# Causal attention heads with on-chip turned probabilities: 32x32 block turns, an on-chip exchange and a plain 32-bit value product

## The chip, the core and the metric

The kernel runs on one core of one Trainium2 chip. A core has TensorE (PE: matmuls and transposes into PSUM), VectorE (DVE), ScalarE (ACT), GpSimd (POOL, which has no access to PSUM) and SyncE (SP), which here only issues DMAs. Each engine runs its own list of instructions in order and waits on semaphores. The metric is the time of one execution on the device, in microseconds (us).

## What is computed

The input `x` has 2 batches of 1024 rows of 256 values. Two blocks follow each other. The first is one causal attention of width 256. The second is a transformer layer: causal attention with 16 heads of width 128 with rotary embedding, and then a mixture of 4 experts of which 2 are taken per row. The part on which the change works is the attention, in both blocks:

```python
scores = jnp.einsum('bhqd,bhkd->bhqk', q, k) / math.sqrt(HD)
scores = jnp.where(causal[None, None], scores, jnp.finfo(jnp.float32).min)
probs = jax.nn.softmax(scores.astype(jnp.float32), axis=-1)
out = jnp.einsum('bhqk,bhkd->bhqd', probs, v)
out = out.transpose(0, 2, 1, 3).reshape(b, s, H * HD)
return out @ wo + bo
```

Everything is 32-bit floating point. In the kernel most products are made of three cheaper ones: each operand is split into a high and a low part of the type `fp32r`, and high x high, high x low and low x high are added up in PSUM.

## The kernel before

The work is cut into 34 units. Units 0 and 1 are the first block's attention for the two batches, units 2 to 33 are one head of one batch each (`unit_of(p, b, h)`: pair of heads, batch, half). A unit has 8 query tiles of 128 rows; tile i needs key tiles 0 to i. So 36 tiles of 128x128 probabilities belong to a unit, and they are treated in two chunks c of 4 query tiles.

For a head unit u the steps are:

- `project_q(u, x)`, x = 0 to 3: TensorE makes queries and keys (two chunks each, 6 matmuls of 512 columns). ScalarE adds the bias (`add_bias`, L1152), SyncE swaps the two halves of the 128 partitions for the rotation with two DMAs (`swap`, L2555 and L2556), VectorE multiplies by the cosine (`rotate`, L1738), GpSimd multiplies by the sine and adds (`turn`, L2296 and L2300), ScalarE writes the high part (`high_qk`, L1158) and GpSimd the low part (`low_qk`, L2307).
- `scores(u, i)`: TensorE, into one or two of the four banks of `ps_s`. VectorE adds the causal mask and takes the maximum (`row_max`, L1777), ScalarE takes the exponential from PSUM into `prob_s` or `prob_b` and its row sum (`exponent`, L1194).
- `transposes(u, i)`: TensorE turns the i + 1 tiles of probabilities, one instruction a tile (L608), into the two banks of `ps_t`. ScalarE copies them out as high part (`high_p`, L1201), VectorE as low part (`low_p`, L1784).
- `outputs(u, c)`: TensorE multiplies the values by the turned probabilities, three matmuls a key tile (12 for chunk 0, 24 for chunk 1). ScalarE and VectorE split the result (`high_o` L1210, `low_o` L1790), `out_project` multiplies it by the output weights (6 matmuls of 256 columns, four times a unit), and VectorE adds it to `acc` (`accumulate`, L1817).
- `project_v(s, g)`: values for the next unit (12 matmuls of 256 columns), split by ScalarE (`high_values`, L1163) and VectorE (`low_values`, L1745).

`take_bank` hands out the two banks of `ps_m` in turn for all but scores and transposes, and waits until the last user's bank has been read.

The order of all this is written out by hand, engine by engine: a `start()` for units 0 to 2, `head(u)` for u = 3 to 30 (28 units, the same list each time, with weight loads that depend on r = (u - 2) mod 4), and an `ends()` for units 31 to 33, the experts and the output. In `head(u)` the scores, maxima and exponents of tiles 4 to 7 of unit u and of tiles 0 to 3 of unit n = u + 1 stand together. TensorE's list in it is:

```python
transposes(u, 0); scores(u, 4); transposes(u, 1); scores(u, 5)
project_q(n, 0); out_project(u - 1, 1, 0)
transposes(u, 2); transposes(u, 3); scores(u, 6)
out_project(u - 1, 1, 1); project_q(n, 1); outputs(u, 0)
transposes(u, 4); project_q(n, 2); out_project(u, 0, 0)
scores(u, 7); transposes(u, 5); out_project(u, 0, 1)
project_q(n, 3); project_v(v_next, 2 * half_of(u)); scores(n, 0)
transposes(u, 6); scores(n, 1); scores(n, 2); scores(n, 3)
transposes(u, 7); project_v(v_next, 2 * half_of(u) + 1); outputs(u, 1)
```

Of the kernel before, what the change touches and what calls it, by code (L numbers as in the profile page):

```python
# [14 lines left out]
P = 128  # L15
BATCH, T, D = 2, 1024, 256
NT = T // P
# [48 lines left out]
VALUES = values_of(LAST) + 1  # L66
QK_JC = ((0, 0), (1, 0), (0, 1), (1, 1))
TG = [[i + 1] if i < 4 else [4, i - 3] for i in range(NT)]
LN_VECTORS = (0, 0, 1, 1, 2, 2)
# [37 lines left out]
def build(nc, A):  # L107

    with ExitStack() as ctx:
# [43 lines left out]
        v_hi = sb("v_hi", [P, 2, NT, D], F32R)  # L153
        v_lo = sb("v_lo", [P, 2, NT, D], F32R)
        pT_hi = sb("pT_hi", [P, NT, CH], F32R)
        pT_lo = sb("pT_lo", [P, NT, CH], F32R)
# [23 lines left out]
        rows = sb("rows", [P, TC, D])  # L180
        hf = sb("hf", [P, KD, CH])
# [25 lines left out]
        t_groups = [(u, i, j) for u in range(UNITS) for i in range(NT) for j in range(len(TG[i]))]  # L207
# [81 lines left out]
        v_hi_done = event("v_hi_done", v_groups)  # L289
        v_lo_done = event("v_lo_done", v_groups)  # L290
# [4 lines left out]
        t_hi = event("t_hi", t_groups)  # L295
        t_lo = event("t_lo", t_groups)
# [74 lines left out]

        def t_bank(u, i, j):
            return ps_t[:, t_mm.place[u, i, j] % 2, :]
# [11 lines left out]
        def we_dst(m, e, n):  # L385
            x = ((qk_hi, qk_lo), (v_hi, v_lo))[m - 1][n]
            whole = x[:, 0].rearrange("p a n -> p (a n)")
            return whole[:, e * CH:(e + 1) * CH]
# [4 lines left out]
        def we2_part(n, e, k):  # L393
            return (v_hi, v_lo)[n][:, 0, 2 * e + k, :]
# [4 lines left out]
        def mid_part(n, u, i):  # L399
            if u == END_MID:  # L400
                return (pT_hi, pT_lo)[n][:, i, :]
# [10 lines left out]
        def m_bank(*use):  # L412
            return ps_m[:, shared[use] % 2, :]
# [15 lines left out]
        def _(pe):  # L429
            freed = {"gate": gate_got, "sums": gate_out, "pv": o_lo, "pvs": acc_done, "wo": acc_done, "mid": gelu_done}  # L430

            def take_bank(*use):

                n = len(shared)
                if n >= 2:
                    kind, *key = list(shared)[n - 2]
                    if kind == "q":
                        empty = first_lo if key[0] < 2 else cos_done
                    elif kind == "v":
                        empty = v_lo_done  # L440
                    elif kind == "ln":
                        empty = hT_hi_act
                    elif kind == "fold":
                        empty = None
                        pe.wait_ge(fold_lo[key[0]], 1)
                    elif kind == "bob":
                        empty = None
# [2294 lines left out]
```

## Time and profile before

| | us |
|---|---|
| median of 3 runs (lowest, highest) | 1116.75 (1116.45, 1118.06) |
| span of the profiled execution | 1115.4 |

The median lies 1.35 us above the profiled span. In the profile, busy times are sums over an engine, "PE" is TensorE's matmuls and "PEld" its weight loads, which run beside them. Matmul records overlap: each lasts from its issue to the end of its pipeline, so what one matmul costs is the distance from its start to the next one's start, not its duration. In a merged row of k equal matmuls the distance is (length of the row - length of one) / (k - 1). A plain 32-bit matmul appears as two records. Which engine waits for which is in the waits at the end of a row, and how the 16 DMA engines are filled is a share of their common time.

### The profile page before, as it was taken

How to read it: one execution, taken by the hardware profiler on the slowest of the kernel's cores; microseconds unless marked ns; L12 is line 12 of the kernel's file. 1: busy time of each engine (PE TensorE's matmuls, PEld its weight loads, DVE VectorE, ACT ScalarE, POOL GpSimd, SP SyncE). 2: the span in 40 equal slices, each digit the busy share in tenths (PEclk: the TensorE clock that was granted, in tenths of full speed). 3: DMA queues.
4: the chain of work that ended last, by engine and by line, in shares of the span. 5: the costliest groups of instructions: out<-in, count | busy, mean ns of one | idle time of the engine just before them, and what ended most of it. 6: DMA issues, size and time to landing. Idle time of an engine off the chain costs nothing.

```text
span 1115.4 us, 20396 instructions
## 1 busy us (share of the span) xinstructions
PE 1105.2 (99%) x7100; PEld 1006.7 (90%) x7100; DVE 834.9 (75%) x1978; ACT 748.3 (67%) x1584; POOL 638.1 (57%) x516
## 2 busy tenths in 40 slices
PE   9999999999999999999999999999999999999997
PEld 8999899999999999999999999999999999988897
DVE  7776777777777777777777777777777777977776
ACT  5666867666666666666666666666666666688765
POOL 2217666555555555555555555555555556777676
PEclk9999999999999999999999999999999999999999
DMA  5002412121212121212121212121211212230102
GB/s 176 1 1 62 129 39 53 39 62 39 52 39 62 39 53 39 60 39 50 37 60 39 52 39 62 39 48 44 62 38 37 50 40 57 48 110 14 39 1 76
DMA packets 33285, 56.54 MB, mean 51 GB/s; under 512 B 5792, under 2 KB 10016, under 8 KB 33184
## 3 DMA queue, kind: packets, MB, share of 16 engines
q1 hardware_dynamic: 33040, 55.21, 19.9%
q8 instruction: 57, 0.93, 0.3%
q14 instruction: 44, 0.36, 0.1%
q10 hardware_dynamic: 144, 0.03, 0.0%
HBM read 17.47 MB, written 4.19 MB: 19 GB/s over the span
## 4 chain that ended last, share of the span: by engine, by line
PE 95%; POOL 2%; issue 1%; ACT 1%; DMA 1%; DVE 1%; SPq 0%; POOLq 0%; ACTq 0%; DVEq 0%
PE ps_m L458 58%; PE ps_s L458 23%; PE ps_t L608 12%; PE ps_m L505 1%; DMA work<-in_attn_w 0%; POOL acc L2341 0%; POOL qk_lo L2346 0%; PE ps_m L479 0%; POOL wqk_lo L2346 0%; PE ps_t L458 0%; POOL pT_lo L2354 0%; DMA work<-work 0%; POOL acc L2330 0%; PE ps_m L666 0%; PE ps_m L667 0%
## 5 line engine op out<-in xcount | busy, mean ns | idle before, releaser
L2296 POOL TENSOR_TENSOR work<-work,rope 128x512 f32<-128x512 f32 x128 | 165.5, 1293 | 222.8 <-DMA work<-work 222.7
L1784 DVE TENSOR_TENSOR pT_lo<-ps_t,pT_hi 128x512 fp32r<-128x512 f32 (+3 forms) x408 | 210.8, 551 | 32.7 <-ACT pT_hi L1201 30.2
L1201 ACT ACTIVATE pT_hi<-ps_t 128x512 fp32r<-128x512 f32 (+3 forms) x408 | 182.8, 489 | 65.3 <-PE ps_t L608 65.1
L1777 DVE CUSTOM_DVE_ANT_0 ps_s<-ps_s,causal 128x128 f32<-128x128 f32 (+7 forms) x272 | 203.5, 767 | 6.7 <-PE ps_s L458 4.1
L2300 POOL TENSOR_TENSOR work<-work 128x512 f32<-128x512 f32 x128 | 167.6, 1310 | 10.0
L2307 POOL TENSOR_TENSOR qk_lo<-work,qk_hi 128x512 fp32r<-128x512 f32 x128 | 163.0, 1293 | 17.8 <-ACT qk_hi L1158 17.8
L1152 ACT ACTIVATE work<-ps_m,bqk 128x512 f32<-128x512 f32 x128 | 88.8, 694 | 116.5 <-PE ps_m L458 116.4
L1817 DVE SCALAR_TENSOR_TENSOR acc<-ps_m,rinv,acc 128x256 f32<-128x256 f32 x272 | 118.6, 478 | 63.0 <-PE ps_m L458 61.7
L1194 ACT ACTIVATE prob_b<-ps_s,nmax 128x640 f32<-128x640 f32 (+3 forms) x136 | 130.3, 958 | 17.9 <-DVE nmax L1777 14.6
L458 PE MATMUL ps_s<-qk_hi 128*128 128x384 f32 (+5 forms) x384 | 140.6, 366 | 0.0
L1738 DVE SCALAR_TENSOR_TENSOR work<-ps_m,bqk,rope 128x512 f32<-128x512 f32 x128 | 95.5, 746 | 54.3 <-ACT work L1152 54.0
L458 PE MATMUL ps_m<-pT_lo,v_hi 128*128 128x512 f32 (+3 forms) x384 | 132.6, 345 | 0.0
L458 PE MATMUL ps_m<-pT_hi,v_lo 128*128 128x512 f32 (+3 forms) x384 | 132.6, 345 | 0.0
L458 PE MATMUL ps_s<-qk_lo,qk_hi 128*128 128x384 f32 (+5 forms) x384 | 131.5, 343 | 0.0
L458 PE MATMUL ps_s<-qk_hi,qk_lo 128*128 128x384 f32 (+5 forms) x384 | 130.9, 341 | 0.0
L458 PE MATMUL ps_m<-pT_hi,v_hi 128*128 128x512 f32 (+3 forms) x384 | 130.1, 339 | 0.0
L608 PE MATMUL ps_t<-ident,prob_b 128*128 128x128 f32 x884 | 120.1, 274 | 0.4 <-DVE pT_lo L1784 0.4
L608 PEld LDWEIGHTS ps_t<-ident,prob_b 128*128 128x128 f32 x884 | 99.7, 140 | 9.8 <-issue 1.2
L458 PE MATMUL ps_m<-hT_hi,wqk_hi 128*128 128x512 f32 x256 | 103.6, 405 | 0.0
L1158 ACT ACTIVATE qk_hi<-work 128x512 fp32r<-128x512 f32 x128 | 79.1, 641 | 36.4 <-POOL work L2300 36.3
L458 PE MATMUL ps_m<-hT_lo,wqk_hi 128*128 128x512 f32 x256 | 101.0, 395 | 0.0
L458 PE MATMUL ps_m<-hT_hi,wqk_lo 128*128 128x512 f32 x256 | 100.5, 393 | 0.0
(235 smaller groups left out, 2822.7 us busy)
## 6 DMA issues: line engine op xcount, KB each, us to landing
work<-work SPq DMA_DIRECT2D x256, 128.0 KB, 2.3
wst<-in_head_qk SPq DMA_DIRECT2D x16, 256.0 KB, 2.9
acc<-in_x_tiles SPq DMA_DIRECT2D x8, 256.0 KB, 6.8
wo_st<-in_L_ffn_wo SPq DMA_DIRECT2D x16, 128.0 KB, 2.4
wst<-in_pair_v SPq DMA_DIRECT2D x8, 256.0 KB, 3.0
x_rows<-acc SPq DMA_DIRECT2D x4, 512.0 KB, 3.6
wst<-in_expert SPq DMA_DIRECT2D x8, 256.0 KB, 3.0
rope<-x_rows SPq DMA_DIRECT2D x4, 512.0 KB, 4.1
```

The lines of the kernel that those rows point to most:

```text
L458: ins = pe.matmul(out, lhs[x], rhs[y], start=first and k == 0, stop=last and k == 2)
L608: last = pe.transpose(t_bank(u, i, j)[:, k * P:(k + 1) * P], probs(i)[:, part], ident[:, :])
L1152: act.activation(qb[:, x % 2, :], m_bank("q", u, x), ACT.Identity, bias=bqk[:, j, head_:head_ + 1]).then_inc(qb_done.sem, qb_done.up(u, x))
L1194: act.activation(probs(i), all_scores[:, score_range(i)], ACT.Exp, bias=nmax[:, u % 2, i:i + 1], scale=-1.0, accum_out=rsum[:, u % 2, i:i ...
L1201: act.activation(pT_hi[:, slots, cols], t_bank(u, i, j)[:, 0:size * P].rearrange("p (j q) -> p j q", q=P), ACT.Copy).then_inc(t_hi.sem, t_ ...
L1738: dve.scalar_tensor_tensor(qc[:, ring3(u, x), :], m_bank("q", u, x), bqk[:, j, head_:head_ + 1], cos_t[:, c * CH:(c + 1) * CH], ALU.add, A ...
L1777: dve.tensor_tensor_reduce(s, s, causal[:, T - (i + 1) * P:T], -1.0, ABOVE_ALL, ALU.add, ALU.min, accum_out=nmax[:, u % 2, i:i + 1]).then_ ...
L1784: dve.tensor_tensor(pT_lo[:, slots, cols], t_bank(u, i, j)[:, 0:size * P].rearrange("p (j q) -> p j q", q=P), pT_hi[:, slots, cols].bitcas ...
L1817: last = dve.scalar_tensor_tensor(acc[:, b, tile, :], src[:, t * D:(t + 1) * D], rinv[:, u % 2, tile:tile + 1], acc[:, b, tile, :], ALU.mu ...
L2296: pool.tensor_tensor(qs[:, x % 2, :], qs[:, x % 2, :], sin_t[:, c * CH:(c + 1) * CH], ALU.mult).then_inc(sin_done.sem, sin_done.up(u, x))
L2300: pool.tensor_tensor(qc[:, ring3(u, x), :], qc[:, ring3(u, x), :], qs[:, x % 2, :], ALU.add).then_inc(rope_done.sem, rope_done.up(u, x))
L2307: pool.tensor_tensor(qk_lo[:, u % 2, j, cols], qc[:, ring3(u, x), :], qk_hi[:, u % 2, j, cols].bitcast(F32), ALU.subtract).then_inc(qk_lo_ ...
```

## The change

For the 28 units of `head(u)` (`TURNED`, u = 3 to 30) the transposes on TensorE go, with the copies that follow them:

- `exponent` writes a row's probabilities stepped: key 128 j + 4 k + g goes to place 128 j + 32 g + k, in runs over g with a step of 32 elements.
- `turn_probs(u, i)`: VectorE transposes each 32x32 block of query tile i (4 (i + 1) blocks per 32 partitions, one instruction a tile) into a buffer `turned[c]`.
- `exchange(u, c)`: SyncE moves the blocks between partitions with four DMAs, from 32 partitions to 128 each: 4 x 256 KB for chunk 0 and 4 x 512 KB for chunk 1, from `turned[c]` to `moved[c]`, 3 MB a unit.
- `early_outputs(u)` (chunk 0) and `far_outputs(u, 0)`, `far_outputs(u, 1)`, `near_outputs(u)` (chunk 1) take the place of `outputs`. Chunk 1 of unit u is multiplied in `head(u + 1)`, or at the head of `ends()` for unit 30.

In all units the value product is one plain 32-bit matmul a key tile instead of three; values and probabilities are no longer split, so `low_p` and `low_values` go, and the copies to SBUF are whole (`copy_p`, `copy_values`). Units 0 to 2 and 31 to 33 still transpose on TensorE. In `head` the two banks of `ps_t` join those of `ps_m`, and `take_bank` takes them in turn. The lists of all engines in `head` are written in another order.

```diff
+            def block_product(u, c, j, last):
+                s, h, off = values_of(u) % 2, half_of(u), max(0, j - TC * c) * Q4
+                out = by_quarter(m_bank("pv", u, c))[:, :, off:P]
+                probs_ = moved[c].rearrange("p (g j n) -> p g j n", g=4, n=P)[:, :, j, off:P]
+                return pe.matmul(out, values[:, s, j, h * HD:(h + 1) * HD], probs_, start=j == 0, stop=last)
+            def far_outputs(u, k):
+                if k == 0:
+                    take_bank("pv", u, 1)
+                    pe.wait_ge(exchanged[1].sem, exchanged[1].at(u))
+                for j in (2 * k, 2 * k + 1):
+                    block_product(u, 1, j, False)
...
+            recent[:0] = [2, 3]
...
+                if by_blocks(u):
+                    to = to.rearrange("p (j g k) -> p j k g", g=4, k=Q4)
+                    scores_ = scores_.rearrange("p (j k g) -> p j k g", g=4, k=Q4)
+                act.activation(to, scores_, ACT.Exp, bias=nmax[:, u % 2, i:i + 1], scale=-1.0,
...
+            def turn_probs(u, i):
+                c = i // TC
+                dve.wait_ge(exp_done.sem, exp_done.at(u, i))
...
+                elif i % TC == 0:
+                    dve.wait_ge(exchanged[c].sem, exchanged[c].at(u - 1))
+                to = turned[c].rearrange("p (g j i q) -> p j i g q", g=4, i=TC, q=Q4)[:, 0:i + 1, i % TC, :, :]
+                blocks = probs(i).rearrange("p (j g k) -> p j g k", g=4, k=Q4)
+                dve.transpose(out=to, in_=blocks).then_inc(turn_done.sem, turn_done.up(u, i))
...
+            def exchange(u, c):
+                sp.wait_ge(turn_done.sem, turn_done.at(u, TC * c + TC - 1))
+                sp.wait_ge(pv_mm.sem, pv_mm.at(u - 1, c))
+                source, to = (x.rearrange("p (g n) -> p g n", g=4) for x in (turned[c], moved[c]))
+                for g in range(4):
+                    sp.dma_start(to[:, g, :], source[g * Q4:(g + 1) * Q4, :, :]).then_inc(exchanged[c].sem, 16)
```

TensorE's list in `head(u)` is now `project_q(n, 0)`, `scores(u, 4)`, `scores(u, 5)`, `project_q(n, 1)`, `far_outputs(u - 1, 0)`, `scores(u, 6)`, `project_q(n, 2)`, `scores(u, 7)`, `far_outputs(u - 1, 1)`, `near_outputs(u - 1)`, `project_q(n, 3)`, `early_outputs(u)`, `out_project(u - 1, 1, 0)`, `scores(n, 0)`, `out_project(u - 1, 1, 1)`, `scores(n, 1)`, `project_v`, `scores(n, 2)`, `out_project(u, 0, 0)`, `scores(n, 3)`, `project_v`, `out_project(u, 0, 1)`.

On TensorE, the end of a `head` before: scores of three tiles, the transposes of tile 7 and the first value projection (`wv`).

```order
L458 MATMUL ps_s<-qk_hi 128x384
L458 MATMUL ps_s<-qk_lo,qk_hi 128x384
L458 MATMUL ps_s<-qk_hi,qk_lo 128x384
L458 MATMUL ps_s<-qk_hi 128x512
L458 MATMUL ps_s<-qk_lo,qk_hi 128x512
L458 MATMUL ps_s<-qk_hi,qk_lo 128x512
L608 MATMUL ps_t<-ident,prob_b 128x128 x8
```

And now, the middle of a `head`: `far_outputs(u - 1, 1)` and `near_outputs(u - 1)` (from `we`, which is `moved[1]`), a projection, and `early_outputs(u)` (from `early_pT`, which is `moved[0]`).

```order
L680 MATMUL ps_t<-we,values 128x512 x3
L680 MATMUL ps_t<-we,values 128x4x96
L680 MATMUL ps_t<-we,values 128x4x64
L680 MATMUL ps_t<-we,values 128x4x32
L493 MATMUL ps_m<-hT_hi,wqk_hi 128x512
L493 MATMUL ps_m<-hT_lo,wqk_hi 128x512
L493 MATMUL ps_m<-hT_hi,wqk_lo 128x512
```

The row with the transposes is gone, the products of a key tile are one row each, and they stand a `head` later than the exponents that feed them.

On VectorE before, from the last maximum of unit u to the split of its values (L1745):

```order
L1777 ISA ps_s,nmax<-ps_s,causal 128x1024
L1777 ISA nmax 128x1
L1784 TENSOR_TENSOR pT_lo<-ps_t,pT_hi 128x4x128
L1784 TENSOR_TENSOR pT_lo<-ps_t,pT_hi 128x2x128
L1777 ISA ps_s,nmax<-ps_s,causal 128x128
...
L1784 TENSOR_TENSOR pT_lo<-ps_t,pT_hi 128x4x128
L1784 TENSOR_TENSOR pT_lo<-ps_t,pT_hi 128x3x128
L1738 SCALAR_TENSOR_TENSOR work<-ps_m,bqk,rope 128x512
L1745 TENSOR_TENSOR v_lo<-ps_m,v_hi 128x512
```

And now, from the same maximum:

```order
L1842 ISA ps_s,nmax<-ps_s,causal 128x1024
L1842 ISA nmax 128x1
L1809 SCALAR_TENSOR_TENSOR work<-ps_m,bqk,rope 128x512
L1857 STREAM_TRANSPOSE pT<-prob_b 128x7x4x32
L1857 STREAM_TRANSPOSE pT<-prob_b 128x8x4x32
L1861 TENSOR_TENSOR oT_lo<-ps_t,oT_hi 128x512
L1809 SCALAR_TENSOR_TENSOR work<-ps_m,bqk,rope 128x512
```

The four reads of `ps_t` became two block turns that wait for ScalarE's exponents, and the split of the last unit's output (`oT_lo`) and a rotation stand behind them.

On SyncE now, one unit with r = 2: the last swap, two weight loads, the exchange of chunk 1, that of the next unit's chunk 0, and the next swap.

```order
L2574 DMA work<-work 64x512
L2575 DMA work<-work 64x512
L2554 DMA wst<-in_head_qk 128x512
L2566 DMA wo_st<-in_L_ffn_wo 128x256
L2583 DMA we<-pT 128x1x1024 x4
L2583 DMA early_pT<-shared_ln 128x1x512 x4
L2574 DMA work<-work 64x512
```

Before, the same swaps followed each other with only the weight loads between them.

## Rows read from the trace of the kernel before

**Rows 1.** The page: span, and each engine's busy time, share and instructions.

```profile
span 1115.4 us, 20396 instructions
PE 1105.2 (99%) x7100; PEld 1006.7 (90%) x7100; DVE 834.9 (75%) x1978; ACT 748.3 (67%) x1584; POOL 638.1 (57%) x516
```

**Rows 2.** The page: engines of the chain of work that ended last.

```profile
PE 95%; POOL 2%; issue 1%; ACT 1%; DMA 1%; DVE 1%; SPq 0%; POOLq 0%; ACTq 0%; DVEq 0%
```

**Rows 3.** Windows: stretch, length, busy by engine, TensorE clock, DMA share, GB/s.

```profile
137.94:929.27 791.33, 791.31 (x5042) 722.07 (x5041) 591.99 (x1315) 524.89 (x1157) 452.97 (x360) 1.00 0.21 47
...
0.00:12.00 12.00, 9.70 (x53) 8.91 (x54) 5.52 (x21) 4.15 (x7) 4.28 (x17) 1.00 0.83 276
```

**Rows 4.** Timeline of TensorE, start, length, operation: first value products of units 2, 30.

```profile
137.94 0.40 PE L458 MATMUL ps_m<-pT_hi,v_hi 128*128 128x512 f32 x1
...
929.27 0.40 PE L458 MATMUL ps_m<-pT_hi,v_hi 128*128 128x512 f32 x1
```

**Rows 5.** Timeline of TensorE in one unit, starts of each kind of work.

```profile
412.81 0.40 PE L458 MATMUL ps_m<-hT_hi,wqk_hi 128*128 128x512 f32 x1
...
414.20 0.28 PE L458 MATMUL ps_m<-wv_hi,hT_hi 128*128 128x256 f32 x1
...
415.63 0.22 PE L458 MATMUL ps_s<-qk_hi 128*128 128x128 f32 x1
...
418.29 1.03 PE L608 MATMUL ps_t<-ident,prob_b 128*128 128x128 f32 x8
419.08 0.38 PE L458 MATMUL ps_m<-wv_hi,hT_hi 128*128 128x256 f32 x1
...
420.60 0.40 PE L458 MATMUL ps_m<-pT_hi,v_hi 128*128 128x512 f32 x1
...
425.21 0.30 PE L608 MATMUL ps_t<-ident,prob_s 128*128 128x128 f32 x1
...
433.70 0.40 PE L458 MATMUL ps_m<-pT_hi,v_hi 128*128 128x512 f32 x1
...
435.57 0.63 PE L608 MATMUL ps_t<-ident,prob_b 128*128 128x128 f32 x4
```

**Rows 6.** Timeline of TensorE at the start: plain 32-bit matmuls, 128 and 256 columns.

```profile
8.44 0.83 PE L464 MATMUL ps_t<-prob_b 128*128 128x128 f32 x6
...
10.68 1.89 PE L479 MATMUL ps_m<-work 128*128 128x256 f32 x8
```

**Rows 7.** The page and groups by form, VectorE: removed groups, and two sizes of one.

```profile
L1784 DVE TENSOR_TENSOR pT_lo<-ps_t,pT_hi 128x512 fp32r<-128x512 f32 (+3 forms) x408 | 210.8, 551 | 32.7 <-ACT pT_hi L1201 30.2
L1784 DVE TENSOR_TENSOR pT_lo<-ps_t,pT_hi 128x512 fp32r<-128x512 f32 x204 | 136.9, 685 | 25.9 <-ACT pT_hi L1201 25.9
L1745 DVE TENSOR_TENSOR v_lo<-ps_m,v_hi 128x512 fp32r<-128x512 f32 x72 | 49.4, 686 | 48.4 <-ACT v_hi L1163 48.2
L1784 DVE TENSOR_TENSOR pT_lo<-ps_t,pT_hi 128x128 fp32r<-128x128 f32 x68 | 19.2, 283 | 4.2 <-ACT pT_hi L1201 4.1
```

**Rows 8.** The page and groups by form, ScalarE: removed copies, and exponents of two sizes.

```profile
L1201 ACT ACTIVATE pT_hi<-ps_t 128x512 fp32r<-128x512 f32 (+3 forms) x408 | 182.8, 489 | 65.3 <-PE ps_t L608 65.1
L1194 ACT ACTIVATE prob_b<-ps_s,nmax 128x1024 f32<-128x1024 f32 x34 | 38.0, 1118 | 2.9
L1194 ACT ACTIVATE prob_s<-ps_s,nmax 128x128 f32<-128x128 f32 x34 | 12.7, 372 | 0.2 <-DVE nmax L1777 0.2
```

**Rows 9.** DMA from 401.3 to 404.3, which holds one swap: packets, queue, landing.

```profile
DMA packets 160, 0.26 MB, mean 87 GB/s; under 512 B 32, under 2 KB 32, under 8 KB 160
q1 hardware_dynamic: 160, 0.26, 41.0%
work<-work SPq DMA_DIRECT2D x2, 128.0 KB, 2.3
```

**Rows 10.** Timelines of SyncE's queue and of GpSimd: a swap, and what follows it.

```profile
406.15 0.46 SPq L2555 DMA_DIRECT2D work<-work  x1
406.65 0.60 SPq L2556 DMA_DIRECT2D work<-work  x1
...
409.08 1.30 POOL L2296 TENSOR_TENSOR work<-work,rope 128x512 f32<-128x512 f32 x1 [1.54 <-DMA work<-work]
...
411.72 2.54 POOL L2307 TENSOR_TENSOR qk_lo<-work,qk_hi 128x512 fp32r<-128x512 f32 x2
```

## What the change does to the time: the prediction

> **What bounds the kernel now.** I read the page first. TensorE is busy for 99% of the span [rows 1] and holds 95% of the chain that ended last [rows 2]. In the 28 units that change, from the first value product of unit 2 to that of unit 30, it is busy 791.31 of 791.33 us at its full clock, 2.4 GHz [rows 3]. Both starts are in [rows 4]: (929.27 - 137.94) / 28 = 28.26 us a unit. So a unit lasts as long as TensorE's list. In the same stretch VectorE works 591.99 / 28 = 21.1 us a unit, ScalarE 18.7, GpSimd 16.2, and the DMA engines 21% [rows 3].
>
> **TensorE's sum.** All by distances between starts.
> - Out, 28 units: 36 transposes. Eight take (1.03 - 0.272) / 7 = 0.108 each, and from 418.29 to the start that follows from the next projection some 0.89 [rows 5], 0.111 each: 4.0 us a unit.
> - Out, head units: three-part value products, 425.21 - 420.60 = 4.61 and 435.57 - 433.70 = 1.87 [rows 5]: 6.48.
> - In: one plain product a key tile, two records of 256 columns each. Eight such records take (1.89 - 0.379) / 7 = 0.216 apart [rows 6], so 1.69 ns a column; a unit has 1280 + 3328 = 4608 columns: 7.77 us. The narrow records support it: (0.83 - 0.275) / 5 = 0.111 for 128 columns [rows 6]. The plain product is dearer than the split one by 1.29 us; only the transposes pay for the change.
> - A unit: 28.26 - 4.0 - 6.48 + 7.77 = 25.55. Times 28: 75.9 us less.
> - Elsewhere: units 2 and 31 to 33 pay 1.29 each, 5.2 us. Units 0 and 1 have 36 products of 256 columns each, 0.432 instead of 3 x 0.119 ((415.63 - 414.20) / 12, [rows 5]): 36 x 0.075 x 2 = 5.4 us.
>
> That gives 1115.4 - 75.9 + 10.6 = 1050.1 us of span, if nothing else is late.
>
> **The other engines' loads.** VectorE loses 210.8 / 34 = 6.2 us and 49.4 / 34 = 1.4 us a unit [rows 7] and gets eight block turns, 4608 elements. No row shows one. The nearest are the removed subtractions: 685 ns at 512 and 283 at 128 [rows 7], or 149 ns + 1.05 ns an element: 8 x 0.149 + 4608 x 0.00105 = 6.0 us. I take this; half of it and twice of it are my bounds. So 21.1 - 7.6 + 6.0 = 19.5 of 25.55. The Trainium skill (Vector Engine (DVE) Microarchitecture Reference, "The reshape front-end and per-opcode configuration") has the transpose sustain one element per cycle per lane; no run here shows it yet, and the sum would stay as it is.
>
> ScalarE loses 182.8 / 34 = 5.4 us [rows 8]: 13.3 left. Exponents cost (1118 - 372) / 896 = 0.83 ns an element [rows 8], 3.8 us a unit. For the stepped write I take no extra; at twice per element it is 3.8 more, 17.1, still under 25.5. The Trainium skill (SBUF — State Buffer, "Door 1: The DMA port swizzle") says that each access to a new 16-byte line pays a penalty, and here each element written is in a new line; it is taken up in rival 2.
>
> SyncE issues 8 more DMAs a unit at 0.5 to 0.6 us [rows 10]: 5 us more, 10 in all. GpSimd keeps 16.2.
>
> **The exchange** is the new transfer: 3.1 MB a unit beside 47 x 28.26 = 1.3 MB. One swap, also from on-chip memory to on-chip memory, moves 0.26 MB in 0.41 x 3.0 x 16 = 19.7 us of DMA engine time [rows 9], so 213 GB/s if all 16 work; the loads at the start ran at 276 / 0.83 = 333 GB/s [rows 3]. I take 213, the same kind of move: 14.8 us a unit, 9.8 for chunk 1 and 4.9 for chunk 0 (9.4 in all at 333). With the swaps the DMA engines are some 82% full.
>
> Hand calendar of a unit (0 = start of `project_q(n, 0)`, which is 414.20 - 412.81 = 1.39 us [rows 5]; scores by their columns): `far_outputs` at 4.7, scores 7 end at 10.4, `project_q(n, 3)` ends at 15.7, `early_outputs` ends at 17.8, scores(n, 0) at 18.5, scores(n, 3) ends at 23.3.
> - Chunk 1: SyncE comes to its exchange only after swap (n, 3), whose bias needs 15.7 + 0.8. With two issues, the swap's own transfer and 9.8 us it lands near 28.8, that is 3.3 in the next unit. `far_outputs` is due at 4.7: slack 1.4.
> - Chunk 0: the last turn ends near 25.7, transfer until 33.3, needed at 41.2: free. But swap (n + 1, 0) is queued behind it on the same queue and lands near 10.2 of its unit instead of 4.5.
> - GpSimd then needs 4 x 1.3 for two turns and 2.54 for two low parts [rows 10], 18.0 to 18.3, and scores(n + 1, 0) wants this at 18.5: slack under 0.5.
> - `out_project(u, 0, 0)` at 21.9 wants `low_o`, which VectorE ends near 21.4, behind two maxima.
>
> In one of four units (r = 2) two weight loads stand ahead of the exchange, 1 us of issues and about 1.5 us of transfer; in one of four (r = 0) three stand ahead of swap (n, 1). By the slacks these cost about 2 and 0.7 us of TensorE. That is (0.7 + 2) / 4 = 0.7 a unit, and near zero if the transfers are a little quicker; between the two I take 0.4: 11 us. At the ends of the chain: unit 3 has no far product to work on while its first exchange is under way (5 us), and the last far product comes first in `ends()` with its exchange still in flight (3 us): 8 us.
>
> Span 1050.1 + 11 + 8 = 1069, and 1.35 outside it, as the median before stands to its profiled span: **1070 us**.
>
> **Rivals.**
> 1. The exchange sets a longer unit (25%). For: the two slacks above are sums of a dozen steps. A transfer 20% slower makes chunk 1 land 2.0 us later, 0.6 past its slack; the late swap adds half of its 3 us, since that loop closes only over two units. About 1.5 us a unit: 1070 + 42 - 11 = 1100.
> 2. Block turns or stepped exponents cost twice (12%). VectorE then has 25.5 of 25.5 and must also wait for the exponents in order; ScalarE has 17.1. I give VectorE's case 1 to 1.5 us a unit: 1087 to 1101. ScalarE's alone costs little: with 0.85 us more for the exponents of tile 7 its turn still ends near 15.5, and the split that follows before 17.8, where `out_project` wants it. The skill's sentence on lines speaks for ScalarE's case, by which the time would be 1070 to 1080.
> 3. Slower than before (9%): the exchange at its place on SyncE's one queue moves less than the swap's rate, and the DMA engines set the unit. The gain is gone when a unit lasts 25.55 + (1115.4 - 1050.1 - 8) / 28 = 27.6 us. Swaps and weights take 1.3 / 0.213 = 6.2 us of it, so the point is an exchange at 3.15 / (27.6 - 6.2) = 147 GB/s, 31% under the swap's rate. At 140 GB/s a unit lasts 6.2 + 22.5 = 28.7 us, and the time is 1050.1 + 8 + 28 x 3.15 + 1.35 = 1148 us. For it: each exchange DMA reads only 32 partitions, and 8 of them a unit were never in flight together. Against it: the swap reads and writes only 64 partitions and both its DMAs overlap [rows 9, 10], and no row is slower.
> 4. No net effect, because gains and stalls cancel within 0.2% (2.2 us, about what a measurement of this kernel can tell from no change): 2%.
> The forecast, TensorE's list with under 1 us of stalls a unit, has 52%: 1048 to 1082.
>
> **Numbers.** Faster 0.89, same 0.02, slower 0.09. Faster is the forecast and rivals 1 and 2. The range runs from no stalls and a short fill (1048) to rival 1 with 2.2 us a unit (1115).
>
> **What the new profile should show.** Plain records 0.215 apart and a unit's TensorE work near 25.6 us; TensorE idle under 3% and put down to the exchange or to `qk_lo`; block turns of 1024 elements near 1.2 us; exponents of 1024 still near 1.12 us; DMA share near 0.8 in the body. A turn above 2 us, an exponent above 2 us or an exchange landing over 12 us after its first issue would prove the step in question wrong; a unit above 27.7 us would undo the gain.

## The result and the profile after

The changed kernel takes **1187.86 us** (median; 1186.4 to 1189.77), the kernel before beside it 1116.92 us (1116.45 to 1118.06). The ratio is **1.0635** with a 95% interval of 1.062 to 1.065: slower by 71 us, where 1070 us, faster by 47, had been forecast, in a range that ended at 1115. The profiled execution has a span of 1184.8 us. Its page, span, busy time, TensorE's clock and the DMA share in 40 slices, and the chain that ended last:

```profile
span 1184.8 us, 17045 instructions
PE 1081.6 (91%) x5636; PEld 869.5 (73%) x5636; DVE 756.2 (64%) x1725; ACT 711.2 (60%) x1248; POOL 634.1 (54%) x516
...
PEclk9999989999999999999999999998999998999999
DMA  4001367676667766776676667666776774221102
...
PE 45%; DMA 19%; SPq 12%; issue 11%; POOL 8%; ACT 4%; DVE 0%; POOLq 0%; ACTq 0%; DVEq 0%
```

Against [rows 1, 2]: TensorE held 95% of the chain and now holds 45%. The DMA engines and SyncE's queue, which held 1% together, hold 31%. The length of a unit can be read from SyncE's timeline (start, length, operation): the first DMA of chunk 1's exchange in unit 3 and in unit 30, and the window between them (busy time by engine, TensorE's clock, DMA share, GB/s).

```profile
167.78 7.60 SPq L2583 DMA_DIRECT2D we<-pT  x4
...
977.29 8.01 SPq L2583 DMA_DIRECT2D we<-pT  x4
...
167.78:977.29 809.51, 728.95 (x3562) 567.98 (x3563) 535.27 (x1107) 470.18 (x790) 430.63 (x345) 0.95 0.69 149
```

(977.29 - 167.78) / 27 = **29.98 us a unit**, against 28.26 before [rows 4] and 25.55 to 25.95 forecast. TensorE stands for a tenth of it, and its granted clock is 0.95 on average, where it was 1.00 [rows 3]. The waits, in all and how often:

```profile
PE ps_t L680 <- DMA we<-pT: 80.3, 27, 4.8
...
DVE pT L1857 <- DMA we<-pT: 37.0, 23, 3.2
```

So TensorE waits once a unit, for chunk 1's exchange, 3 us each time on average. The engines that were in doubt do their work at these prices (groups by form: count, then busy time and mean ns of one, then idle time ahead):

```profile
L1266 ACT ACTIVATE prob_b<-ps_s,nmax 128x1024 f32<-128x1024 f32 x34 | 65.4, 1922 | 12.0 <-DVE nmax L1842 11.9
...
L1857 DVE STREAM_TRANSPOSE pT<-prob_b 128x1024 f32<-128x1024 f32 x28 | 34.9, 1246 | 14.8 <-ACT prob_b L1266 14.8
```

The turn is as estimated (149 + 1024 x 1.05 = 1224 ns forecast, 1246 measured). The stepped exponent is not: 1922 ns against 1118 [rows 8].

**One unit, followed back.** The chain of waits of the changed kernel from one far product to the next (start, length, what):

```profile
630.17 3.34 PE ps_t L680 x4
633.51 1.49 PE ps_s L493 x6
635.01 1.38 PE ps_m L493 x6
636.38 1.36 PE ps_s L493 x6
637.74 3.87 PE ps_t L680 x12
641.61 1.40 PE ps_m L493 x6
...
643.04 0.70 ACT work L1217
...
643.75 0.46 SPq L2574
...
644.25 0.60 SPq L2575
...
644.95 0.59 SPq L2583
...
646.24 3.91 SPq L2583
...
650.20 9.60 DMA we<-pT
...
659.93 2.39 PE ps_t L680 x4
```

The rows from the first far product to the start of the next, 659.93 - 630.17, are a closed loop of 29.76 us. `far_outputs(u - 1, 0)` is followed by scores, projections and `project_q(n, 3)` on TensorE (643.01 - 630.17 = 12.8 us). Then come the bias on ScalarE, the two DMAs of swap (n, 3), and only then, since SyncE works in order, the exchange of chunk 1, which lands 14.85 us after its first issue and lets the next far product start. There is no exponent and no block turn in it; the last turn of this unit (VectorE, L1857) ends at 642.48, 2.5 us before the exchange's first issue. The third issue takes 3.91 us, where the first took 0.59. The trace does not show what it waits for; two transfers of 512 KB are under way at that time.

Around the wait TensorE's timeline reads:

```profile
626.94 0.40 PE L493 MATMUL ps_t<-hT_hi,wqk_lo 128*128 128x512 f32 x1
630.17 3.34 PE L680 MATMUL ps_t<-we,values 128*128 128x512 f32 x4 [2.84 <-DMA we<-pT]
632.52 1.36 PE L493 MATMUL ps_s<-qk_hi 128*128 128x448 f32 x1
```

and the windows of TensorE's clock behind it, of the exchange as a whole, and of two stretches of it:

```profile
630.20:633.50 3.30, 3.30 (x5) 1.43 (x6) 0.78 (x1) 0.00 (x0) 0.00 (x0) 0.56 0.84 223
...
644.95:659.80 14.85, 12.53 (x86) 11.53 (x85) 11.41 (x30) 11.08 (x21) 8.23 (x7) 1.00 0.94 184
...
647.00:649.00 2.00, 2.00 (x18) 2.00 (x17) 1.87 (x9) 1.72 (x5) 1.92 (x2) 1.00 0.85 119
...
649.00:653.00 4.00, 4.00 (x31) 3.83 (x30) 3.54 (x10) 3.91 (x9) 3.05 (x3) 1.00 0.99 189
```

After 2.84 us without work TensorE runs at a mean of 0.56, that is nearly all at 1.2 GHz, and only then back at 2.4 GHz. So this wait is paid for twice. It is not so in every unit: in the 2.3 us from the start of the far product the clock is 0.50 to 0.80 in 20 of the 27 units with a wait, behind waits of 2.35 to 4.77 us, and 1.00 in the other seven, behind waits of 0.68 to 2.73 us. The two groups overlap, so the length of the wait alone does not decide it.

### The profile page after: what moved, and what is told of

The parts are those of the page before. It is cut to its first block, busy times and chain, and to the rows that moved or that the text cites. A ratio compares the mean times of both kernels' runs of the same rounds, so it can differ in the third digit from the quotient of the medians.

```text
span 1184.8 us, 17045 instructions
## 1 busy us (share of the span) xinstructions
PE 1081.6 (91%) x5636; PEld 869.5 (73%) x5636; DVE 756.2 (64%) x1725; ACT 711.2 (60%) x1248; POOL 634.1 (54%) x516
## 4 chain that ended last, share of the span: by engine, by line
PE 45%; DMA 19%; SPq 12%; issue 11%; POOL 8%; ACT 4%; DVE 0%; POOLq 0%; ACTq 0%; DVEq 0%
DMA we<-pT 18%; PE ps_m L493 13%; PE ps_t L680 12%; PE ps_s L493 12%; SPq L2583 9%; POOL work L2314 2%; POOL work L2318 2%; PE ps_m L656 2%; PE ps_m L672 2%; POOL qk_lo L2325 2%; PE ps_t L643 2%; ACT work L1217 1%; SPq L2575 1%; SPq L2574 1%; PE ps_m L680 1%
## 5 line engine op out<-in xcount | busy, mean ns | idle before, releaser
L1266 ACT ACTIVATE prob_b<-ps_s,nmax 128x640 f32<-128x640 f32 (+3 forms) x136 | 219.5, 1614 | 221.4 <-DVE nmax L1842 221.1
L680 PE MATMUL ps_t<-we,values 128*128 128x512 f32 (+3 forms) x432 | 186.1, 578 | 80.3 <-DMA we<-pT 80.3
L680 PEld LDWEIGHTS ps_t<-we,values 128*128 128x128 f32 x432 | 84.8, 202 | 159.9 <-issue 149.2
L1857 DVE STREAM_TRANSPOSE pT<-prob_b 128x640 f32<-128x640 f32 (+1 forms) x112 | 116.6, 1041 | 54.1 <-DMA we<-pT 37.0
L1266 ACT ACTIVATE prob_s<-ps_s,nmax 128x128 f32<-128x128 f32 (+3 forms) x136 | 108.2, 807 | 11.2 <-DVE nmax L1842 9.6
L493 PEld LDWEIGHTS ps_s<-qk_hi 128*128 128x128 f32 x384 | 77.1, 201 | 23.1 <-issue 17.1
L493 PEld LDWEIGHTS ps_s<-qk_lo,qk_hi 128*128 128x128 f32 x384 | 76.0, 198 | 15.6 <-issue 11.1
L1223 ACT ACTIVATE qk_hi<-work 128x512 fp32r<-128x512 f32 x128 | 80.3, 629 | 11.2 <-POOL work L2318 10.8
L1282 ACT ACTIVATE oT_hi<-ps_t 128x512 fp32r<-128x512 f32 x55 | 32.9, 598 | 89.9 <-PE ps_m L493 89.9
L1888 DVE SCALAR_TENSOR_TENSOR acc<-ps_m,rinv,acc 128x256 f32<-128x256 f32 x160 | 67.6, 464 | 24.4 <-PE ps_m L656 15.8
L493 PEld LDWEIGHTS ps_s<-qk_hi,qk_lo 128*128 128x128 f32 x384 | 75.2, 196 | 5.5
```

Of the source, the lines that this page charges most:

```text
L493: ins = pe.matmul(out, lhs[x], rhs[y], start=first and k == 0, stop=last and k == 2)
L680: return pe.matmul(out, values[:, s, j, h * HD:(h + 1) * HD], probs_, start=j == 0, stop=last)
L1223: act.activation(qk_hi[:, u % 2, j, c * CH:(c + 1) * CH], qc[:, ring3(u, x), :], ACT.Copy).then_inc(qk_hi_done.sem, qk_hi_done.up(u, x))
L1266: act.activation(to, scores_, ACT.Exp, bias=nmax[:, u % 2, i:i + 1], scale=-1.0, accum_out=rsum[:, u % 2, i:i + 1]).then_inc(exp_done.sem, ...
L1857: dve.transpose(out=to, in_=blocks).then_inc(turn_done.sem, turn_done.up(u, i))
```

## The experiments

Theory L (loop): the exchange of chunk 1, with its place on SyncE's list, closes the loop above. Its rivals: the stepped exponents or VectorE's order (E), a TensorE that is itself slower than summed, the DMA engines' capacity.

### One part at a time

**Exponents in plain order.** The three lines `if by_blocks(u): to = ...; scores_ = ...` in `exponent` are gone.

> The changed kernel with the exponents of all units written in plain order; all else is as it was, and the output is no longer the reference's because the keys then stand in the wrong places. Theory L (loop): the unit of 29.9 us is set by a loop through TensorE, ScalarE's bias, SyncE's list and the exchange of chunk 1; from the end of one projection project_q(n, 3) (643.01) to the landing of the exchange (659.80) it has no exponent in it. Then the exponents fall back to 1.12 us at 1024 elements, ScalarE gets 3 to 4 us a unit of idle time more, and the time stays within 0.5% of 1187.9 us. Theory E (engines): the stepped exponents hold up the turns and through them everything else; then 1 to 3.8 us a unit come back, 1080 to 1160 us.

Measured: 1189.4 us. The exponents did get cheap again:

```profile
L1263 ACT ACTIVATE prob_b<-ps_s,nmax 128x1024 f32<-128x1024 f32 x34 | 37.9, 1116 | 30.9 <-DVE nmax L1839 30.9
```

ScalarE waits for maxima instead. The exponents' part of theory E is out for this kernel; VectorE's part is met by the next run.

**Half of chunk 1's bytes.**

```diff
+                part = slice(0, T // 2) if c == 1 and u > TURNED[0] else slice(None)
                 for g in range(4):
-                    sp.dma_start(to[:, g, :], source[g * Q4:(g + 1) * Q4, :, :]).then_inc(exchanged[c].sem, 16)
+                    sp.dma_start(to[:, g, part], source[g * Q4:(g + 1) * Q4, :, part]).then_inc(exchanged[c].sem, 16)
```

> The changed kernel, but in units 4 to 30 each of the four DMAs of the exchange of chunk 1 moves half of its bytes (256 KB instead of 512 KB); the other half of the turned probabilities is left out, and the products read old ones. The number of DMAs, waits and matmuls is the same. Theory L: the issues of SyncE block for less, the exchange lands 7 to 8 us earlier, and TensorE's list sets the unit: 1067 to 1080 us, the gap at far_outputs gone. If instead the number of DMAs or their place in SyncE's list decided, and not the bytes, the time would stay above 1150.

Measured: **1065.24 us**, 2 us under the range given. With the same number of DMAs, waits and matmuls 123 us are gone. One unit's four issues on SyncE, and the window of the body:

```profile
608.17 4.93 SPq L2584 DMA_DIRECT2D we<-pT  x4
...
150.00:900.00 750.00, 738.32 (x3820) 592.10 (x3820) 563.90 (x1171) 503.68 (x849) 459.58 (x369) 1.00 0.59 131
```

The issues take 4.93 us instead of 7.77, and TensorE keeps its full clock. The block turns, the plain product, VectorE's order and everything else that this kernel shares with the changed one can't be what makes a unit last 30 us. But the run lowers the load of the DMA engines too (share 0.59 instead of 0.69), so it does not part theory L from the engines' capacity. The runs below that move all bytes do.

**The plain product alone.** In the kernel before, `product(...)` of values and probabilities becomes one `pe.matmul`, and `low_p` and `low_values` go.

> One part of the change alone in the kernel before: values and probabilities are not split, the value product is one plain 32-bit matmul a key tile; TensorE still transposes all tiles, no block turns, no exchange, the old order of the lists without the low parts. By the sum of the prediction TensorE, which is busy for 99% there, gets 1.29 us more in each of 32 units and 2 x 2.7 us in the first two: 1116.9 + 41.3 + 5.4 = 1163.6 us. If the plain product costs more than its rows at the start said, it comes above 1175; if VectorE's 7.6 us less a unit helped anything, below 1155.

Measured: 1158.24 us, +41.3 where the sum said +46.7. TensorE is busy in 800.00 of 800.00 us of its body, so this is a clean reading of TensorE's list: the term was 5 us too high. By the starts of the first value products of units 2 and 30, 142.41 and 965.27, a unit lasts 29.39 us, 1.13 more than before, where 1.29 had been summed.

**The far product later.** `far_outputs(u - 1, 0)` moves from before `scores(u, 6)` to behind `scores(u, 7)`.

> The changed kernel with far_outputs(u - 1, 0) moved behind scores(u, 7) in TensorE's list. Theory L: the way from the product that waits to project_q(n, 3) becomes 5 us shorter, so this loop no longer sets the unit, TensorE's gap of 2.8 us before the far product closes and with it the stretch at 1.2 GHz. A second loop then decides: SyncE's list, exchange of chunk 1, exchange of chunk 0, and swap (n + 1, 0) behind both, then GpSimd's two turns and two low parts before scores(n + 1, 0); by the profile of the change it lasts about 27.4 us, which gives 1187.9 - 28 x 2.5 = 1118 us; if it overlaps better, down to TensorE's list, 1187.9 - 28 x 4.3 = 1067 us. Theory E or a TensorE that is itself slower: the time stays within 1% of 1188.

Measured: 1151.27 us: faster than the changed kernel, but by 37 us instead of 70. The gap before the far product is gone, another stands in its place. SyncE's timeline and the wait:

```profile
625.00 7.85 SPq L2582 DMA_DIRECT2D we<-pT  x4
633.02 6.91 SPq L2582 DMA_DIRECT2D early_pT<-shared_ln  x4
640.05 0.80 SPq L2573 DMA_DIRECT2D work<-work  x1
...
PE ps_s L493 <- POOL qk_lo L2324: 50.7, 27, 5.4
```

This is the second loop. The swap of the next unit's first projection is issued only when both exchanges have been handed over, 15 us after the first DMA of chunk 1; GpSimd's turns and low parts follow, and scores(n + 1, 0) waits for them. It had been put at 27.4 us, and it lasts 28.55 (same reading as above).

### Two loops

**Swap ahead of chunk 0, alone and with each cure of the first loop.** In SyncE's `head`:

```diff
                 if by_blocks(n):
+                    swap(n + 1, 0)
                     exchange(n, 0)
```

> The changed kernel with one step of SyncE's list moved: swap(n + 1, 0) is issued before exchange(n, 0) instead of behind its four DMAs. Theory L: the first loop (TensorE's list, bias, swap, exchange of chunk 1) stays as it is, only that chunk 0 starts some 3 us later and takes less of the DMA engines while chunk 1 is still under way; chunk 1 lands 0.5 to 1.5 us earlier, 1145 to 1174 us, and GpSimd's wait for the swap of 11 us gets shorter. If the late swap were what sets the unit of the changed kernel, the time would fall below 1120.

Measured: 1192.3 us, a miss: nothing gained. The exchange from its first issue to its landing, in the window view:

```profile
622.70:637.52 14.82, 12.54 (x86) 11.54 (x85) 11.14 (x30) 10.35 (x20) 8.32 (x7) 1.00 0.92 177
```

Chunk 0 was issued at 636.32 here, practically behind it, and chunk 1 still took 14.82 us. So what I had thought, that chunk 1 lands sooner when chunk 0 no longer takes its share, is wrong. 14.82 x 177 = 2.62 MB is chunk 1 (2.10) and two swaps (0.52).

> Both moves: far_outputs(u - 1, 0) behind scores(u, 7), and swap(n + 1, 0) before exchange(n, 0). All bytes are moved as in the changed kernel. Theory L with its two loops: the first is cut by 5 us and the second (exchange of both chunks, swap, GpSimd, scores) by 6 to 7 us, so that TensorE's list of 25.6 us sets the unit: 1065 to 1085 us, and TensorE keeps its full clock. Rival B (bytes): the DMA engines, which work some 20 us a unit, can't be filled better than about three quarters, and the unit stays above 27 us: over 1105 us.

Measured: 1148.41 us, a miss: hardly better than the far product's move alone. GpSimd now idles one step later too, between the turns of x = 0 and x = 1 (3.4 and 4.3 us in two units that follow each other), because swap (n + 1, 1) still stands behind chunk 0; scores wait for `qk_lo` as before (56.1 us in 27 waits).

**The exchange of chunk 1 in two halves.** Key tiles 0 to 3 first, on their own semaphore:

```diff
+                for n in range(c + 1):
+                    part, there = slice(n * CH, (n + 1) * CH), (far_there if n < c else exchanged[c])
+                    for g in range(4):
+                        sp.dma_start(to[:, g, part], source[g * Q4:(g + 1) * Q4, :, part]).then_inc(there.sem, 16)
```

> TensorE's order as in the changed kernel; swap(n + 1, 0) before exchange(n, 0), and the exchange of chunk 1 in eight DMAs of 256 KB: first the key tiles 0 to 3, on which far_outputs now waits alone, then 4 to 7, on which near_outputs waits. The same bytes in 4 DMAs more. Theory L: the first half lands near the middle of the old transfer, 6 us earlier, before TensorE comes to it; both loops are off the path, 1065 to 1085 us. Rival I (issues): each DMA's own cost on SyncE's queue counts and not its bytes; then nothing is gained over the same kernel without the split, above 1140 us.

Measured: **1096.27 us**, ratio 0.9815 (0.9789 to 0.9842): all bytes moved, four DMAs more, and faster than the kernel before by 1.6 to 2.1%, though 11 us above the range given.

> The split of chunk 1's exchange alone: eight DMAs of 256 KB, key tiles 0 to 3 first, far_outputs waits for these only; SyncE's order as in the changed kernel (the next swap behind both exchanges). Theory L with two loops: the first goes, TensorE's gap and its stretch at 1.2 GHz with it, the second (both exchanges, the late swap, GpSimd, scores) stays and gives what moving far_outputs gave, 1140 to 1155 us. If the split alone did it all in the kernel with split and swap ahead, the time is again 1090 to 1100 us.

Measured: 1104.6 us, ratio 0.9881. The split alone brings 83 us; I had expected 33 to 48 and was wrong on the second loop, which lasts 27.22 us here and not the 28.55 of the moved far product.

**Both swaps ahead.** As above, with `swap(n + 1, 1)` ahead of `exchange(n, 0)` too.

> As the kernel with the split and swap(n + 1, 0) ahead of exchange(n, 0) (1096 us), but swap(n + 1, 1) stands ahead of it too. In the profile of that kernel GpSimd idles 3.4 to 4.2 us between the turns of x = 0 and x = 1, for a swap that SyncE issues only behind chunk 0. Theory L: this wait goes, scores(n + 1, 0) no longer waits for qk_lo (31.7 us in 18 waits), and TensorE's list sets the unit: 1065 to 1080 us. Rival: chunk 0 now starts 3 us later and early_outputs comes to wait for it, or the DMA engines are simply full; then 1090 or above.

Measured: **1059.50 us** (1059.17 to 1060.95), ratio **0.9483** (0.9469 to 0.9497), where 1065 to 1080 was expected. Page, chain, and the window of the 27 units between the same two issues as above:

```profile
PE 1039.6 (98%) x5636; PEld 852.4 (81%) x5636; DVE 754.5 (71%) x1725; ACT 713.3 (67%) x1248; POOL 635.8 (60%) x516
...
PE 88%; POOL 4%; issue 3%; ACT 2%; DMA 1%; SPq 1%; DVE 0%; POOLq 0%; ACTq 0%; DVEq 0%
...
167.88:857.22 689.34, 689.06 (x3559) 551.81 (x3559) 533.50 (x1106) 472.25 (x790) 433.16 (x345) 1.00 0.77 175
```

689.34 / 27 = **25.53 us a unit**, TensorE busy in 689.06 of 689.34 us at full clock. The prediction's sum for TensorE's list was 25.55. The same bytes as in the changed kernel keep the DMA engines 77% busy in a unit that is 4.4 us shorter, so their capacity did not set the changed kernel's unit.

### Where the swaps are issued

**Swaps on ScalarE's queue**, in the changed kernel and with the split; SyncE keeps the exchanges for itself. In ScalarE's `head`:

```diff
                 exponent(u, 7)
+                swap(n, 2)
                 high_qk(n, 0)
...
                 add_bias(n, 3)
+                swap(n, 3)
```

> The changed kernel with the swaps of its 28 units issued by ScalarE on its own queue, each one or two steps behind its add_bias; the exchanges keep SyncE's queue for themselves. All bytes as before. Theory L: exchange(u, 1) no longer stands behind swap(n, 3) and starts with the last turn, 2.5 us earlier, and the swaps of x = 0 and 1 no longer stand behind SyncE's blocked issues. The loop then goes exchange, far product, scores 6 and 7, exponents, turns: about 27.4 us, or 1187.9 - 28 x 2.5 = 1118 us (range 1100 to 1140). Rival Q: the order on the queue doesn't matter since the DMA engines are full with chunk 1 anyway; then the swaps land as late as now and the time stays above 1160.

Measured: **1342.9 us**, ratio 1.2025: 155 us slower than the changed kernel instead of 70 faster, the largest miss. Timelines of ScalarE's queue, GpSimd and ScalarE, and the wait:

```profile
670.98 0.51 ACTq L1226 DMA_DIRECT2D work<-work  x1
...
671.52 3.48 ACTq L1227 DMA_DIRECT2D work<-work  x1
...
684.29 1.26 POOL L2327 TENSOR_TENSOR work<-work,rope 128x512 f32<-128x512 f32 x1 [10.21 <-DMA work<-work]
...
686.93 0.63 ACT L1232 ACTIVATE qk_hi<-work 128x512 fp32r<-128x512 f32 x1 [7.97 <-POOL work L2331]
...
PE ps_s L493 <- POOL qk_lo L2338: 211.2, 28, 8.7
```

Swap (n, 3), issued 1.3 us behind the start of chunk 1's exchange, lets GpSimd go on only 13.3 us after its first issue; a swap's DMA on SyncE's queue lands in 2.4 (median, changed kernel). It now shares the engines with 2.1 MB instead of preceding them. GpSimd stands for it, ScalarE's `high_qk(n, 3)` behind GpSimd, and `exponent(n, 3)` and the next unit's work behind that. The second issue holds ScalarE itself for 3.48 us; what that adds no run tells apart. The Trainium skill (DMA: Bandwidth & Descriptors, "Issuing engines are not separate DMA queues") says that DMAs of all issuing engines run on the same 16 DMA engines and interleave; the trace agrees. It adds that the time saved on the sequencer is usually small beside the DMA itself; here an issue takes 0.59 us on a free queue and 3.91 us on a full one.

> Both: the swaps on ScalarE's queue and the exchange of chunk 1 split into key tiles 0 to 3 and 4 to 7. Theory L: no loop is longer than TensorE's list, 1065 to 1080 us. Rival: eight more issues on ScalarE (0.5 to 0.6 us each, 4.4 us a unit) and its waits for GpSimd hold up the exponents; then 1090 or above.

Measured: 1122.98 us, again a miss, 18 us above the split with the swaps on SyncE (1104.6), with the same kind of waits (`qk_lo`: 53.4 us in 32). The place of swap (n, 3) ahead of the exchange on one queue, which had looked like a fault, was what kept it quick.

### The clock

**Work for TensorE ahead of the wait.**

```diff
                 if k == 0:
-                    take_bank("pv", u, 1)
+                    out = take_bank("pv", u, 1)
+                    for i in range(11):
+                        pe.matmul(out, hT(0, 0, slice(0, P))[0], hT(0, 0, slice(0, CH))[0], start=True, stop=True)
```

> The changed kernel with 11 matmuls of 512 columns that nobody needs (2.5 us) on TensorE just ahead of its wait for the exchange of chunk 1, into the bank that the product then overwrites. It tests whether the fall to 1.2 GHz behind the wait is a result of the wait. If TensorE falls to half of its clock because it stood for 2.8 us, the stretch of 3.4 us at 1.2 GHz goes and with it 1.7 us of each unit, as it lies inside the loop: about 1187.9 - 27 x 1.6 = 1145 us, clock near 1.00. If the fall has another cause (the plain product itself, or power), the clock stays at 0.96 and the time at 1188 or above. If there is no loop and TensorE's own work sets the unit, the time rises by 28 x 2.5 to 1258 us.

Measured: 1160.49 us, clock 0.995. Eleven useless matmuls a unit make the kernel 27 us **faster**. TensorE's timeline:

```profile
614.62 2.67 PE L694 MATMUL ps_t<-hT_hi 128*128 128x512 f32 x11
617.13 1.88 PE L680 MATMUL ps_t<-we,values 128*128 128x512 f32 x4
```

The four records of the far product take 1.88 us, where they took 3.34 behind the wait; between 617.3 and 619.0 the clock is 1.00. The gain is 27.4 / 27 = 1.0 us a unit, less than the 1.6 expected: TensorE still waits for the exchange, 13.3 us in all, in 15 of the units, and in the others the filler outlasts the old wait. The Trainium skill (TensorE: Matmul & The Clock Gate, "HAM oscillation") tells of a loop in which TensorE waits for a DMA in each pass and starts each pass at the lower clock. The trace of the changed kernel agrees for 20 of 27 units: 0.56 behind the wait of 2.84 us shown above, 1.00 here with the wait filled.

### Rival 2, once nothing else is in the way

Both kernels start from the one of 1059.5 us.

> The kernel with chunk 1's exchange split and two swaps ahead of chunk 0 (1059.5 us), with the exponents of all units written in plain order; the output is not the reference's, since the keys then stand in the wrong places. ScalarE loses 3 to 4 us a unit of 17. Theory L says that TensorE's list sets the unit there and neither engine is near it: within 0.5% of 1059.5. If ScalarE's longer way to the last turns held anything up, 0.3 to 0.8 us a unit come back: 1037 to 1051.

Measured: 1060.85 us. ScalarE's 3.8 us a unit lie beside TensorE's list and cost nothing.

> The same kernel (1059.5 us) with every block turn of the 28 units done twice, the second behind the first: 8 instructions and 6 us a unit more on VectorE, some 25.5 us of 25.6 in all. That is the condition of the prediction's rival with turns at twice their cost. By that rival it costs 1 to 1.5 us a unit, 1088 to 1101; if VectorE's order is loose enough, under 1070; if its waits for the exponents and the scores come on top of a full engine, over 1130.

Measured: 1084.66 us, +25.2 us or 0.9 us a unit, 3 us under the rival's range. VectorE's window:

```profile
150.00:900.00 750.00, 724.77 (x3695) 575.01 (x3694) 704.38 (x1371) 478.60 (x819) 447.92 (x357) 0.99 0.74 167
```

VectorE is busy for 94% of it, and a unit lasts 26.4 us. That a full VectorE lengthens the unit is shown (the prediction's rival said by 1 to 1.5 us); the rival's condition, turns at twice the price, was not met in the changed kernel.

### The order of the source partitions

```diff
-                for g in range(4):
+                for g in (0, 2, 1, 3):
```

> The changed kernel with the four DMAs of each exchange issued in the order g = 0, 2, 1, 3 instead of 0, 1, 2, 3; nothing else. Theory P (paths): neighbours in the old order read the same half of the 128 partitions (0 to 31 and 32 to 63) and hinder each other; in the new order two halves are read at once, the 3.9 us of the third issue get shorter and chunk 1 lands 2 to 3 us earlier. Since the loop through it sets the unit of 29.98 us, all of this comes off each unit: 1105 to 1135 us. Rival: the packets' rate doesn't depend on which partitions two DMAs in flight read; 1180 to 1195 us and 14.8 us to the landing as before.

Measured: **1135.99 us**, 52 us less than the changed kernel, with nothing but the order of four DMAs; a unit lasts 28.25 us. The windows of the body, changed kernel first, then this one, with TensorE's wait for the exchange (80.3 us in 27 waits in the changed kernel) and two stretches of one exchange:

```profile
150.00:900.00 750.00, 672.34 (x3300) 525.37 (x3298) 498.13 (x1033) 437.05 (x735) 399.45 (x319) 0.95 0.69 149
```

```profile
150.00:900.00 750.00, 695.17 (x3463) 546.29 (x3462) 526.02 (x1083) 461.54 (x770) 419.63 (x335) 0.97 0.68 158
...
624.40:626.40 2.00, 2.00 (x18) 2.00 (x18) 1.87 (x9) 1.66 (x5) 1.92 (x3) 1.00 0.92 72
626.40:630.40 4.00, 4.00 (x31) 3.83 (x30) 3.54 (x10) 3.91 (x9) 3.31 (x3) 1.00 0.94 223
...
PE ps_t L680 <- DMA we<-pT: 47.8, 24, 4.1
```

For the time that the DMA engines are busy they move 149 / 0.69 = 216 GB/s before and 158 / 0.68 = 232 after. The Trainium skill (SBUF — State Buffer, "Door 1: The DMA port swizzle") has partitions 0 to 31 and 32 to 63 reach the same half of the DMA ports; the gain from not reading them one behind the other agrees. But the gain is not where and not as large as I put it. The third issue still takes 4.38 us in this unit, the first stretch is not faster (72 GB/s where 119 were moved), only the next one is (223 instead of 189), and the exchange lands 14.75 us after its first issue, no sooner than in the changed kernel. Over all units it does: from the first issue to the far product's start it is 14.0 us in the mean of the 25 units in which TensorE waits (12.9 to 15.5), and 15.1 in the changed kernel's 28 (14.1 to 16.1). So 1.1 us a unit came where 2 to 3 had been expected; that the unit is 1.7 us shorter fits a clock that falls less (0.97 instead of 0.95). How two such DMAs hinder each other stays open.

> The kernel of 1059.5 us (split, two swaps ahead of chunk 0) with each group of four DMAs in the order g = 0, 2, 1, 3. TensorE's list sets its unit of 25.53 us, so a faster exchange buys nothing: within 0.3% of 1059.5 by theory L, whatever theory P gives the transfer. If the exchange still held anything up there, up to 5 us less.

Measured: 1057.91 us (1057.50 to 1058.99), ratio 0.9471 (0.9457 to 0.9485), the lowest median of the study, though this interval overlaps that of the kernel of 1059.5 us. The DMA share of the body falls from 0.74 to 0.68 at the same 169 GB/s, and the time hardly moves, as TensorE's list sets it.

## Why the prediction was wrong, step by step

- **TensorE's list, 25.55 us a unit: right, in part by luck.** 25.53 was measured where nothing else is late. Even the whole sum of 1050.1 with 8 us for the ends and 1.35 outside the span, 1059.5 us without stalls, is what that kernel takes. But two terms were off and cancelled: the plain product costs 1.13 us a unit and not 1.29, and by difference the transposes gave back 29.39 - 25.53 = 3.86 us and not 4.0.
- **Block turns: right. Stepped exponents: the price was wrong, the effect right.** I took no extra; they take 1.7 times as long at 1024 elements (twice per element: (1922 - 1116) / 1024 = 0.79 ns more on 0.83). It cost nothing in either kernel. The Trainium skill (SBUF — State Buffer, "Door 1: The DMA port swizzle") says that each access to a new 16-byte line pays a penalty; a dearer stepped write agrees with it, though no run here varies the step, so that the lines are the reason is not shown.
- **The exchange of chunk 1: the step that failed.** "With two issues, the swap's own transfer and 9.8 us it lands near 28.8 ... slack 1.4" is 11.2 us from the first issue of the exchange; 14.85 were measured, 3.65 more. The 9.8 came from 213 GB/s, read from one swap [rows 9] as bytes over busy share. Two DMAs of 128 KB that start on empty engines are no measure of eight queued ones of 256 or 512 KB. The stretch moved 184 GB/s at a share of 0.94, the swaps around it included, and chunk 1's own bytes 2.10 / 14.85 = 141 GB/s. Nor did the calendar have an issue that takes 3.91 us. An estimate from these numbers: the stretch moved 14.85 x 184 = 2.73 MB, and at 213 GB/s that is 12.8 us. So 1.6 of the 3.65 us are bytes that the calendar did not have in this stretch, and 2.0 a lower rate. Why the rate is lower no run settles; the order of the source partitions has a part in it.
- **The price of being late: the second failure.** Rival 1 saw this wait and gave it about 1.5 us a unit at 20% less speed, as if it happened in some units only or were half absorbed. Its own numbers, 0.6 past the slack and 1.5 for the late swap, would be 2.1 if both count. It is a loop: the late far product delays `project_q(n, 3)`, this the swap, this the exchange. The calendar has it at 25.55 - 1.4 = 24.15 us; it lasts 29.76. Of the 5.6 us more 3.65 are the exchange, and 1.8 are TensorE between the start of the far product and the end of `project_q(n, 3)`: 12.8 us instead of 15.7 - 4.7 = 11.0, since part of it runs at half the clock, for which the prediction had no term. In the kernel of 1059.5 us, at full clock, the same stretch takes 11.0 (614.19 to 625.17). In the mean of the units TensorE stands for 80.3 / 27 = 3.0 us and is busy for (728.95 - 689.06) / 27 = 1.5 us more than in that kernel: 25.5 + 3.0 + 1.5 = 30.0.
- **Rival 3 had the sign and not the mechanism.** It said that below 147 GB/s the gain would be gone, and 141 is below, by coincidence: 141 is chunk 1's bytes over the whole time to its landing, issues and swaps included, and 147 was a rate of full DMA engines. The rival had the DMA engines' capacity as the bound. They are 69% busy, and at 77% the same bytes go with a unit of 25.53 us. It is the time from first issue to landing that counted, and the place where the product waits.
- **The second slack, swap (n + 1, 0) behind chunk 0, was real** and cost nothing as long as the first loop was longer: removing it alone gave 1192 us. Once the first loop was cut, this swap ahead of chunk 0 was worth 8 us (1104.6 to 1096.27), and swap (n + 1, 1) ahead of it too another 37 (to 1059.5).
- **The signs.** Of the three that the prediction named for a wrong step one came, an exchange that lands over 12 us after its first issue (14.85); an exponent of 1024 elements stayed just under its sign of 2 us (1.92).
- **The chances.** 9% on slower was too little for a schedule that rested on two slacks of 1.4 and 0.5 us behind a transfer of a size that no row showed.

## What to carry to other kernels

When a step is moved to another engine and comes back by DMA, draw the ring through the transfer and ask how long it is from first issue to landing; the share of busy time of the DMA engines gave no warning here, and what exceeds the slack is paid in every pass. Let the consumer wait for the part that it needs first (here four DMAs of eight), and put small urgent transfers ahead of large patient ones on the same queue; here a second queue made it worse (1188 to 1343 us). A slack that is shorter than the uncertainty of the transfer in it is no slack.

## What the hardware showed unexpectedly

- An issue on SyncE's queue took 0.59 us on a free queue, and 3.9 us as the third of 512 KB; everything behind it on that queue waited too.
- A wait of 2.84 us on TensorE was followed by a stretch at a mean clock of 0.56, and the clock fell in 20 of the 27 units with a wait; useless matmuls in the wait's place gained 27 us.
- The order in which four DMAs read their quarters of the partitions was worth 52 us where the exchange was on the path.
- ScalarE's exponential with an output step of 32 elements takes 1922 ns at 1024 elements and 1118 without. VectorE's block turn, which writes runs of 32 elements, takes 1246.
